# Two routed down products ahead of the last shared gate product, and an earlier turn of queries in an attention loop

## The reference

```python
logits = x @ router_w
expert_idx = argmax(logits); score = sigmoid(max(logits)); xs = x * score
out[rows of e] = (silu(xs @ gate_w[e]) * (xs @ up_w[e])) @ down_w[e]
shared = silu(x @ shared_gate_w) * (x @ shared_up_w) @ shared_down_w
result = out + shared
```

```python
scores = einsum(q, k) / sqrt(8); attn = softmax(scores); out = attn @ v; result = out @ Wo + bo
```

## Time and profile before

| | |
|---|---|
| median of three runs | 669.4 us (667.64 to 670.4) |
| profiled execution, its own time | 665.62 us |
| its span, first to last instruction | 663.9 us, mean granted PE clock 0.983 |
| PE busy | 615.3 us (93%) |
| DVE busy | 400.0 us (60%) |
| ACT busy | 328.4 us (49%) |
| POOL busy | 208.7 us (31%) |
| share of PE on the chain that ended last | 76% |
| share of DVE on it | 15% |

### The profile page before, as it was taken

How to read it: one execution, slowest core, us unless ns; L and a number is a source line. 1 busy time by engine, 2 the same in 40 slices (tenths; PEclk the granted TensorE clock), 3 DMA queues, 4 the chain that set the end, 5 groups by cost and what they waited for, 6 DMA issues and landing times.

```text
span 663.9 us, 11796 instructions
## 1 busy us (share of the span) xinstructions
PE 615.3 (93%) x4298; PEld 407.6 (61%) x4298; DVE 400.0 (60%) x929; ACT 328.4 (49%) x654; POOL 208.7 (31%) x304
## 2 busy tenths in 40 slices
PE   3999999999999988999879999999999999999980
PEld 2887887888888785566566444444444445556650
DVE  5426705632760577443377989888899955743335
ACT  4523423433332234254315588898988875423321
POOL 5870661282074064313422122111010100431331
PEclk9999999999999999999979999999999999999995
DMA  6100200300199996314199996000000000031213
GB/s 221 33 1 33 96 1 25 102 1 1 34 272 271 119 176 223 105 48 120 69 296 335 270 155 4 1 2 1 2 1 2 1 2 1 17 106 47 84 53 126
DMA packets 69000, 57.40 MB, mean 86 GB/s; under 512 B 21520, under 2 KB 64400, under 8 KB 68944
## 3 DMA queue, kind: packets, MB, share of 16 engines
q1 hardware_dynamic: 66736, 50.60, 34.0%
q0 software_dynamic: 2208, 6.05, 2.5%
HBM read 30.78 MB, written 25.85 MB: 85 GB/s over the span
## 4 chain that ended last, share of the span: by engine, by line
PE 76%; DVE 15%; ACT 3%; DMA 2%; issue 2%; POOL 2%; ACTq 0%; POOLq 0%; SPq 0%; DVEq 0%
PE psum L303 9%; PE psum L305 9%; PE psum L304 9%; PE psum L1296 8%; PE psum L1641 8%; DVE mx L1751 7%; PE psum L1325 5%; PE psum L1613 5%; PE psum L1601 5%; PE psum L1626 3%; PE psum L1289 3%; DVE stat L652 2%; PE psum L1220 2%; PE psum L1571 2%; PE psum L1305 1%
## 5 line engine op out<-in xcount | busy, mean ns | idle before, releaser
L1751 DVE TENSOR_REDUCE mx<-psum 128x1 f32<-128x512 f32 x256 | 157.7, 683 | 17.5 <-PE psum L1613 17.4
L1512 ACT ACTIVATE pr<-psum 128x512 f32<-128x512 f32 x256 | 137.8, 599 | 28.2 <-PE psum L1626 26.4
L1641 PE MATMUL psum<-pr,vals 128*32 128x256 f32 x1024 | 77.6, 389 | 0.0
L1626 PE MATMUL psum<-qT,kT 32*128 32x512 f32 x256 | 76.5, 494 | 0.7 <-ACT pr L1512 0.7
L1613 PE MATMUL psum<-kT,qT 32*128 32x512 f32 x256 | 67.7, 489 | 1.7 <-ACT qT L1479 0.7
L1296 PE MATMUL psum<-w_gu,xgT 128*128 x120 | 56.4, 592 | 0.0
L610 POOL DMA_INDIRECT routed_y<-yr,xg x30 | 28.8, 958 | 87.8 <-DVE yr L862 87.2
L1613 PEld LDWEIGHTS psum<-kT,qT 32*128 32x128 f32 x256 | 26.3, 182 | 43.9 <-issue 21.0
L1553 POOL CAST mp<-mx 128x16 bf16<-128x16 f32 x16 | 3.1, 196 | 150.6 <-DVE mx L1751 150.6
L853 DVE SCALAR_TENSOR_TENSOR h<-psum,xg,sg 128x256 f32<-128x256 f32 x30 | 14.5, 484 | 49.8 <-ACT sg L1051 49.8
L999 ACT ACTIVATE q<-psum 128x512 f32<-128x512 f32 x32 | 19.1, 596 | 48.9 <-PE psum L305 48.9
(11 more groups left out here) (214 smaller groups left out, 1391.7 us busy)
## 6 DMA issues: line engine op xcount, KB each, us to landing
sorted_x<-zeros SPq DMA_DIRECT2D x2, 9088.0 KB, 45.3
w_gu<-in_L_ffn_gate_w SPq DMA_DIRECT2D x16, 256.0 KB, 6.3
w_gu<-in_L_ffn_up_w SPq DMA_DIRECT2D x16, 256.0 KB, 6.4
w_d<-in_L_ffn_down_w SPq DMA_DIRECT2D x16, 256.0 KB, 6.2
xg<-sorted_x SPq DMA_DIRECT2D x30, 129.0 KB, 2.2
wk_f<-in_L_attn_Wk SPq DMA_DIRECT2D x4, 512.0 KB, 5.2
wq_f<-in_L_attn_Wq SPq DMA_DIRECT2D x4, 512.0 KB, 5.9
wv_f<-in_L_attn_Wv SPq DMA_DIRECT2D x4, 512.0 KB, 3.9
```

The lines of the kernel that those rows point to most:

```text
L1512: nc.scalar.activation(pr[d % 3][:, j], s2_bank(d, j), ACT.Exp, scale=SCALE).then_inc(exp_ready, 1)
L1626: mm(s2_bank(d, j), kT[n // GH][rows, kc * P:(kc + 1) * P], qT2[n % 2][rows, :], start=True, stop=True).then_inc(s2_made, 1)
L1641: last = mm(ps[AV_BANK][j * VW:(j + 1) * VW, cols], vals[:, n // NKV * TB + kc, n % NKV // GH * GH + j, :], pr[d % 3][:, j, cols], start=( ...
L1751: v.tensor_reduce(mx[n % 2][:, t, j:j + 1], s1_bank(c, j), AX.X, ALU.max, negate=True).then_inc(max_read, 1)
```

## The change

In the mixture, at i = 22 (`NU - 1`), down(20) and down(21) on PE now stand between turn_h(21) and gate_up(22); on DVE take_down(20) and take_down(21) stand ahead of gated(22). ACT's program isn't changed. In the attention, `turns_at` gives q1 at c % 4 == 0 instead of c % 4 == 2, listed ahead of "o", and no turn at c % 4 == 2. The same function places the instructions on PE, the copies on ACT and the items in the rings, so all of them move together. The number of instructions, DMAs and bytes stays the same.

```diff
             for i in range(3, NU + 1):
+                if i == NU - 1:
+                    for u in downs_at(i):
+                        take_down(u)
                 if i < NU:
                     gated(i)
-                for u in downs_at(i):
-                    take_down(u)
+                if i != NU - 1:
+                    for u in downs_at(i):
+                        take_down(u)
...
                 if i == NU - 1:
                     turn_h(i - 1)
+                    for u in downs_at(i):
+                        down(u)
                 if i < NU:
                     gate_up(i)
...
-                for u in downs_at(i):
-                    down(u)
+                if i != NU - 1:
+                    for u in downs_at(i):
+                        down(u)
...
             if c % TB == 0:
-                what = ("o", (c - 12) // TB)
+                what = [("q1", c // TB + 1), ("o", (c - 12) // TB)]
             elif c % TB == 1:
-                what = ("q2", (c - 5) // TB)
-            elif c % TB == 2:
-                what = ("q1", c // TB + 1)
+                what = [("q2", (c - 5) // TB)]
+            elif c % TB == 3:
+                what = [("k", (c + 5) // 16 if (c + 5) % 16 == 0 else NG)]
             else:
-                what = ("k", (c + 5) // 16 if (c + 5) % 16 == 0 else NG)
-            return [what] if 0 <= what[1] < (NKT if what[0] == "k" else NG) else []
+                what = []
+            return [x_ for x_ in what if 0 <= x_[1] < (NKT if x_[0] == "k" else NG)]
```

## The result

The kernel took 660.12 us in the median of 4 runs (659.58 to 663.84), the kernel before beside it 668.76 (667.64 to 670.4, 4 runs). The ratio is 0.9861, 95% interval 0.9829 to 0.9894: 8.6 us faster, where 7.5 were forecast. The profiled execution of the changed kernel took 660.29 us, its span is 658.6 us. That is only 5.3 less than the profiled execution of before (665.62), so the two comparisons don't agree, and part of this text is about the difference.

A forecast was written before the change was run, and what follows sets the result against it. PE was on the chain for most of the span, with routed tiles waiting behind an unneeded gate product and PE and DVE waiting on each other in attention; 3.4 + 4.1 = 7.5 us off 669.4 gives 661.9, range 657.8 to 668.3.

The forecast's parts named there:

- Part 1, 2 x 1.72: End of both mixtures: down(20) no longer waits for unit 22's shared gate product, 1.72 us gained each, 3.44 together.
- The cover of 1.4 for y_shared: First mixture: y_shared, made later by the change, is still done 1.4 us before the routed rows' load lands.
- Part 2, the plain period: Attention groups without a k turn: o turn to o turn falls from 11.31 to 10.93 us, ten gains of 0.38.
- the last group: Attention loop's last group, without a q1 turn in its third step; the new period of 10.93 us was worked out from it.
- Part 2, the k groups: Three attention groups with a k turn: 11.75 us falls to 11.52, 0.23 gained each, 0.7 in all.
- The copy on ACT at no cost: Attention, first step: ACT's moved q1 copy fits where ACT waits for PE's scores2, so it costs nothing.
- The start of the loop: Attention at c = 0, 4 and 8: moved turns enter steps already full, costing 0.4 us, bounds 0 to 1.8.
- Rival 1: Attention loop gives nothing, the q1 turn being paid in full at its new place: 666.0 us, chance 0.17.
- Rival 2: Attention: ACT's ring takes over and the kernel is slower, 673.7 us at full price; chance 0.04.
- Rival 4: Attention: PE and DVE decouple better, the loop gains near 0.59 us a group, 658.3 us; chance 0.08.
- Rival 3: Clock falls between the filler matmuls and attention's projections, a cold start losing 2.3 us: 664.2 us, chance 0.09.
- Sum: Whole kernel: 3.4 us from the mixtures plus 4.1 from the attention loop, 7.5 in all.

The follow-up runs named there:

- the edit on PE alone: Changed kernel with DVE gating unit 22 first, as before the change, ahead of taking down products 20 and 21: 667.73 us, ratio 0.9954 to the kernel before.
- The quarter turn: Kernel before with one transpose instead of four in each q1 turn from group 3 on, still in the third step: 669.54 us, ratio 1.0005.
- the refilled third step: Changed kernel with 0.64 us of PE matmuls added in each group's third step, c = 10 to 58: 669.72 us, ratio 1.0027 to the kernel before.
- the last series: Runs on one chip of q1 in the fourth step, the edit on PE alone and the changed kernel again (660.79 us); the kernel before took 670.76.
- the middle series: Runs on one chip of q1 behind o, no q1 and the refilled third step; the kernel before, run beside them, took 666.52 us.
- q1 behind o: Changed kernel with PE making the q1 turn right behind the o turn, still in the first step: 665.45 us, ratio 0.999 to the kernel before.

## Why the prediction was right

- *Part 1, 2 x 1.72.* Measured 1.69 at both scatters in the first mixture; 1.56 was left at rstd, and 1.68 at the start of the second load. What is missing in the first is no more than the landing varies: from the transposes to rstd it is 18.99 to 19.44 in six traces without the edit, and 17.46 to 18.17 in six with it. The cover of 1.4 for y_shared was 1.36. The forecast had moved take_down on DVE without giving it a price of its own; the edit on PE alone shows what hangs on it: without it, 1.7 us gained become 1.6 lost.
- *Part 2, the plain period.* 10.93 by PE was forecast, 10.86 by DVE; measured 10.86 to 10.92, ten plain periods together 4.07 shorter, and 10.88 without any q1. The step that counted was to read the last group, which has no q1 turn in its third step. Ten gains of 0.41 instead of 0.38.
- *Part 2, the k groups.* Forecast 11.52, measured 11.45: k costs 0.55 and not the whole 0.59 of its turn. Three gains of 0.28 instead of 0.23.
- *The copy on ACT at no cost.* It stood at 446.25 in the hole of the first step, and ACT still waited 0.22 for PE behind it. Right.
- *What I had read too simply* is why the old place was dear. I put it down to PE's 0.59. The quarter turn shows that with half of PE's time gone the item in ACT's ring (place and copy) still holds the period near 11.3. Whether PE's time alone would hold it there too isn't shown: the refilled third step had q1's work in the first. Leaving the item out wholly frees the period, and so does moving all of it. The forecast held because the last group lacks all of it, not because of the reason that I gave.
- *The start of the loop.* 0.4 forecast, 0.67 measured, within 0 to 1.8. The 0.4 was a choice and not worked out. It was too little by 0.27, and the gains of the groups were too little by 0.41, so that part 2 came out at 4.24 beside 4.1: the small errors partly cancel.
- *Rival 1* (the loop gives nothing) fell by the period. *Rival 2* likewise. *Rival 4* fell too: DVE's stop at the second step is still there, and a group gains 0.41, not 0.59. *Rival 3*, a cold start of the attention: the clock fell beside the layernorm again, though PE now stood still only from 332.61 to 334.91, and was back where it was, before the attention's projections (windows, columns as above; compare).

```profile
333.50:334.00 0.50, 0.00 (x0) 0.00 (x0) 0.00 (x0) 0.00 (x0) 0.00 (x0) 0.64 0.80 254
340.00:340.50 0.50, 0.50 (x4) 0.50 (x4) 0.50 (x3) 0.00 (x0) 0.00 (x0) 0.54 1.09 365
```

- *Sum.* 7.5 forecast; 7.5 by the trace's steps, 7.7 at equal clock, 8.6 by the first medians. I put the us beyond the forecast down to the granted clock: it is gone between runs of equal clock, and none of the ten runs of the changed kernel had a mean clock under 0.983. That it fell in the loop in the slower runs of before is argued from five other kernels' profiles; both profiles of before have 1.00 throughout the loop.

**What stays open.** Whether the change itself makes these falls rarer. For it: none of the 16 runs of the changed kernel and of the mixture's edit alone had a mean clock under 0.983, while 24 of the 29 runs of before beside that edit had, 13 of the 17 in the last series, and all 12 of the attention's edit alone. Against it: only 6 of the 19 runs of before in the middle series had; and the changed kernel with q1 behind o and with its third step refilled has the mixture's edit too, and both show a fall at 375 to 390 us in their profiles (granted clock 0.50 in 380 to 385 in both). No run here moves the fall by itself. What the late slot computation waits for was not settled either; the trace calls it remote. Nor was it settled whether the edit of the mixture brings the long last part of the first load: 4.09, 4.33 and 4.61 are three of the four first mixtures that have both the whole edit and the late slot computation, and no other mixture has one.

## What to carry to other kernels

- A move from a full place to one where the engine waits gains what the full place cost, if all that the item holds moves with it: engine time, ring bank and copy. Half of the engine time alone, taken away, gained next to nothing here. Look for an iteration of the same loop that happens to lack the item (the last, the first) and read the new period from it.
- Where one engine produces and another takes in program order, change both orders or none. Half of this edit was worth 3.3 us less per mixture than the whole.
- Before a difference of medians is laid to an edit, compare executions of equal granted clock, and compare a stretch that both kernels share word for word. The mean alone doesn't say where the clock was low: the kernel with the refilled third step has a fall in the loop at a mean of 0.983, the kernel before has none at 0.983.

## What the runs showed of the hardware

- The granted clock can fall to 1.2 GHz for part of 10 us in a loop in which PE was busy 4.05 of the 5 us before, and not in another execution with the same instructions there: in the attention's edit alone 0.64 and 0.68 in two windows of 5 us; in the changed kernel, whose attention program is the same, 1.00 in both, with PE busy 4.45 before. The weigh products then took 1.86 instead of 1.00 us. In the last series the seven executions of before with a mean clock of 0.974 to 0.976 took 4.4 us more than the four at 0.984 or 0.985 (medians 672.9 and 668.5).
- The same wait of one DVE instruction was 0.60 to 0.64 us in the four profiles of one series and the first of before, and 3.09 to 3.34 in the eight others. From the first half's slot computation to the transposes of unit 21 a mixture took 64.32 to 64.34 us in the former and 64.92 to 65.60 in the latter.
- The last part of the load of the routed rows took 2.6 to 3.2 us in 23 of 26 mixtures, and 4.09, 4.33 and 4.61 in three, with the same bytes.
